# Moving the second attention's first tanh and a row turning into the last feed-forward chunk, and the way out of that chunk to another PSUM bank

## The chip, the cores and the metric

One NeuronCore of a Trainium2 chip runs the whole program. The metric is the device time of one execution in microseconds (us), as the median of several runs; smaller is better. The engines are named as the profile names them: PE (TensorE matmul), PEld (its weight loads), ACT (ScalarE), DVE (VectorE), POOL (GpSimd) and SP (SyncE, which issues the DMAs). Each engine works through its own instruction list strictly in the order in which the kernel wrote it, and engines meet only at semaphores.

## The reference

Input x is 2 x 1024 rows of 128. Four blocks follow one another, each of the form `x = x + layernorm(block(layernorm(x)))`:

1. block A, causal attention of one head with rotary embedding;
2. block B, a feed-forward of width 512: `h = silu(x w1) * (x w2)`, `h = gelu(h h1)`, `h = gelu(h h2)`, `out = h w3`, each product with a scale per output column;
3. block C, the second attention, of 8 heads, with two score maps L1 and L2 for each head:

```
G  = tanh(gain * (L1 - L2))
A1 = softmax(L1 + G)
A2 = softmax(L2 - G)
y  = rmsnorm((A1 - lambda * A2) @ v) * weight;  out = y @ Wo.T + bo
```

4. block D, a feed-forward with 8 routed experts.

## The kernel before, in words

Everything is written out by hand, engine by engine; no planner reorders anything. The 2048 rows are 16 tiles of 128, in 4 chunks of 512.

**Block B** runs over chunks c = 0 to 3. PE makes the first pair of products (L761), the product with h1 (L780), and the product with h2 (L790). The h2 product has four output tiles o = 0 to 3, each summed over k = 0 to 3 and each in PSUM bank o. ACT takes each tile o out with a Gelu (L1101, semaphore `g2_b`). Then `b_out_tile` (L747) multiplies with w3, one of four row tiles k4 at a time (T0 to T3 below), and DVE takes the four out together with `b_evac` (L1393, semaphore `yo_b`). For the last chunk the four tiles stand among the first products of block C, in bank 6. `c_prep_turn` turns the normed rows of chunk 2 for block C's projections and `c_evac` (ACT, L1047) takes them out of the turning bank, bank 7.

**Block C** is 128 steps, s = 0 to 127 (16 pairs of batch and head, n, by 8 key tiles, mt). A step consists of

- D(s), `c_diff`: two products of gain * q and k into banks 0 and 1, which give gain * (L1 - L2). It waits for tanh(s-1), which empties the banks;
- tanh(s), `tanh_step` on ACT, L1117, out of banks 0 and 1. It waits for D(s);
- F(s), `c_first`, into banks 2 and 3, and S(s), `c_second`, into banks 4 and 5: the two score maps. They wait for Zf(s-1) and Zs(s-1);
- Zf(s), `z_first` on DVE, L1486, adds tanh(s) to F(s), and Zs(s), `z_second`, L1491, takes tanh(s) from S(s), both into one of two halves of `zz`;
- exp(s) on ACT, L1146, 2048 columns of `zz`, waits for Zs(s);
- V(s), `c_values` on PE, L693: eight products of exp(s) with v, summed in bank 6. It waits for exp(s).

F, S and D all stand at L674 in the profile. The order within the loop of step s is, on PE, `D(s+3), turning, F(s+2), V(s), S(s+2)`; on ACT, `tanh(s+2), exp(s)`; on DVE, `Zf(s), Zs(s)` and then other work of that step. A preamble on PE fills the pipe. In the kernel before it reads, after the h2 product of the last chunk: `D(0), F(0), S(0), c_prep_turn(2), T0, D(1), T1, D(2), F(1), T2, S(1), T3`. ACT does, after the last Gelu, a small Exp (which brings the load of another function table, L1133), tanh(0), `c_evac(2)`, tanh(1), and then the loop.

`SPECIAL` is a table of further work in bank 7, by (n, mt). PE makes it before F(s+2) of that step, and DVE takes it out at the end of the following step (`turn_out`, L1505 for the kind "raw"). DVE's own list has `b_evac(3)` in step 1 and `b_stats(3)` (L1248 and L1251, four tiles each) in step 2. V(0) waits for `b_evac(3)`, since both use bank 6.

SP issues the loads of head 0 in the order q_g, k_s, q_s (semaphore `load[0]`), k_w, q_w (`cross[0]`), two DMAs each. D(0) waits for `load[0]`.

Of the kernel before, what the change touches and what calls it, by code (L numbers as in the profile page):

```python
# [27 lines left out]
BT = SEQ // P  # L28
# [41 lines left out]
SPECIAL = {(0, 2): ("raw", 0), (0, 5): ("raw", 1), (1, 1): ("v", 0), (1, 3): ("sums", 0), (2, 1): ("scale", 0),  # L70
# [72 lines left out]
def sandwich(nc, x_in, a_w, rope, b_w12, b_h1, b_h2, b_w3, b_s, b_s3, c_w, c_wo, c_bo, small,  # L143
             d_wg, d_wu, d_wd, d_wr, ident_in, ident_bf_in, mask_in, before_in, out):
    with ExitStack() as ctx:
# [342 lines left out]
        def _(pe):  # L488
# [128 lines left out]
            def c_turning(use):  # L617
# [3 lines left out]
                if kind == "o":  # L621
                    pe.wait_ge(S["accout"], i + 1)
                    last = turn_chunk(acc_sb.rearrange("p (a b) -> p a b", a=CT))
                elif kind == "late turn":
                    pe.wait_ge(S["xn_c"], CHUNKS)
                    last = turn_chunk(xn_c)
                elif kind == "raw":
                    if i == 0:
                        pe.wait_ge(S["xt_c"], CHUNKS - 1)
                    last = c_raw(i % 2, turn)  # L630
                elif kind == "v":
                    last = c_v()
                elif kind == "sums":
                    pe.wait_ge(S["sq_c"], CHUNKS - 1 + i)
                    last = c_sums(turn)
                elif kind == "scale":
                    pe.wait_ge(S["fac_c"], CHUNKS - 1 + i // 2)
                    last = c_scale(i % 2, turn)
                elif kind == "y":
                    pe.wait_ge(S["yc"], i + 1)  # L640
                    last = turn_chunk(y_c[i % 2])
                elif kind == "wo":
                    if i == 0:
                        pe.wait_ge(S["small_c"], 1)
# [106 lines left out]
            pe.wait_ge(ld["bw"], 48)  # L751
            for c in range(CHUNKS):
# [32 lines left out]
                for o in range(KT_):  # L785
                    pe.wait_ge(S["g1_b"], KT_ * c + o + 1)
                    for k in range(KT_):
                        if o == 0:
                            pe.wait_ge(S["g1_b"], KT_ * c + k + 1)
                        last = mm(ps[:, o, :], w_h2[:, k, o * P:(o + 1) * P], hid[:, 1, k, :],  # L790
                                  start=(k == 0), stop=(k == KT_ - 1))
                    last.then_inc(S["m2_b"], 1)
                    if 1 <= c < CHUNKS - 1:
# [62 lines left out]
            pe.wait_ge(load[0], 16 * OWN)  # L856
            late_c = CHUNKS - 1
            pe.wait_ge(S["g2_b"], KT_ * late_c + 2)
            c_diff(0, 0, 0)
            pe.wait_ge(cross[0], 16 * CROSSED)  # L860
            pe.wait_ge(S["g2_b"], KT_ * CHUNKS)
            c_first(0, 0, 0)
            pe.wait_ge(S["yo_b"], late_c)
            c_second(0, 0, 0)
            c_prep_turn(late_c - 1)
            pe.wait_ge(S["qh_c"], 2)
            b_out_tile(late_c, 0, ps[:, 6, :])
            c_diff(1, 0, 1)
            b_out_tile(late_c, 1, ps[:, 6, :])
            c_diff(2, 0, 2)  # L870
            c_first(1, 0, 1)
            b_out_tile(late_c, 2, ps[:, 6, :])
            c_second(1, 0, 1)
            b_out_tile(late_c, 3, ps[:, 6, :]).then_inc(S["y_b"], 1)
            for n in range(NH):
                for mt in range(BT):
                    s = n * BT + mt
                    later = s + 2 < NH * BT
# [19 lines left out]
                    if mt == 0:  # L898
                        pe.wait_ge(S["vh"], n + 1)
                        pe.wait_ge(S["accout"], n)  # L900
                        if n == 0:
                            pe.wait_ge(S["yo_b"], CHUNKS)
                    c_values(s, n % 2, mt)
                    if later:
                        c_second(s + 2, n2 % 2, mt2)

# [37 lines left out]
        def _(act):  # L944
# [129 lines left out]

            act.wait_ge(ld["bw"], 48)
            me.mark(A(tiny[:, 57:58], s_b[:, 0:1], ACT.Silu))
            for c in range(CHUNKS):
# [19 lines left out]
                for o in range(KT_):  # L1097
# [3 lines left out]
                    A(hid[:, 2, o, :], ps[:, o, :], ACT.Gelu, scale=s_b[:, 12 + o:13 + o]).then_inc(S["g2_b"], 1)  # L1101
                    if 1 <= c < CHUNKS - 1:
# [9 lines left out]

            def tanh_step(s, u, mt):
                act.wait_ge(S["dd"], s + 1)
                if s >= 3:
                    act.wait_ge(S["z2"], s - 2)
                A(gg[s % 3], banks[:, 0:2 * CHUNK], ACT.Tanh).then_inc(S["g"], 1)  # L1117
# [16 lines left out]
            tanh_step(0, 0, 0)  # L1134
            c_evac(CHUNKS - 2)
            tanh_step(1, 0, 1)
            for n in range(NH):
                for mt in range(BT):
                    s = n * BT + mt
                    if s + 2 < NH * BT:  # L1140
                        n2, mt2 = divmod(s + 2, BT)
                        tanh_step(s + 2, n2 % 2, mt2)
                    act.wait_ge(S["z2"], s + 1)
                    if s == NH * BT - 1:
                        act.wait_ge(S["av"], s - 1)
# [66 lines left out]
        def _(dve):  # L1212
# [435 lines left out]
            for n in range(NH):  # L1648
                u = n % 2
                for mt in range(BT):  # L1650
                    at = (n, mt)
                    z_first(n * BT + mt, mt)
                    if mt == 1 and n:
                        acc_out(n - 1)
                    z_second(n * BT + mt, mt)
                    if at == (0, 1):
                        b_evac(CHUNKS - 1, ps[:, 6, :])
# [5 lines left out]
                    if at == (0, 2):  # L1663
# [446 lines left out]
```

## Time and profile before

| what | value |
|---|---|
| median of 3 runs | 700.99 us (700.08 to 701.39) |
| the profiled execution, its time | 701.4 us |
| its span (first to last instruction) | 699.6 us |
| mean granted TensorE clock | 0.997 |
| PE busy | 633.5 us, 91% of the span |
| DVE busy | 529.0 us, 76% |
| ACT busy | 489.2 us, 70% |
| POOL busy | 188.2 us, 27% |

The profile shows one execution; times in it count from the first instruction. The execution took 701.4 us around a span of 699.6 us, so 1.8 us lie outside the span. The last chunk of block B ends on PE at about 234.1 us, and block C's steps run from there to about 599 us.

### The profile page before, as it was taken

The numbers are of one execution on the slowest core, as the hardware profiler recorded it, in microseconds if no ns is written. First come the engines' busy times: TensorE is split into PE (matmuls) and PEld (weight loads), VectorE is DVE, ScalarE is ACT, GpSimd is POOL, SyncE is SP. The second block draws the span as 40 slices with busy tenths as digits, with TensorE's granted clock in tenths as the row PEclk, the third lists the DMA queues.
The fourth block names the chain that finished last, engine by engine and source line by source line (L and its number), as shares of the span: only waits on it lengthen the run. The fifth ranks groups of instructions, "written<-read, shape, count | busy, mean of one in ns | idle before, by whom it ended". The sixth has DMA issues, their size and how long they took to land.

```text
span 699.6 us, 9403 instructions
## 1 busy us (share of the span) xinstructions
PE 633.5 (91%) x3324; PEld 272.5 (39%) x3324; DVE 529.0 (76%) x993; ACT 489.2 (70%) x504; POOL 188.2 (27%) x250
## 2 busy tenths in 40 slices
PE   8899999999999999889988888898898778899996
PEld 4677445464464423223321212122232111266555
DVE  5877603327054399999899999999999999676775
ACT  4657424234333699999999999999999989444432
POOL 3532340112102042491138101705500006022012
PEclk9999999999999999999999999999999999999999
DMA  6340200002205310244013420121101103300171
GB/s 172 102 171 1 92 1 0 2 0 72 64 1 147 101 33 26 57 115 135 9 49 111 138 58 21 37 57 57 38 20 58 56 3 121 120 1 1 47 226 30
DMA packets 33231, 44.60 MB, mean 64 GB/s; under 512 B 5409, under 2 KB 20001, under 8 KB 32801
## 3 DMA queue, kind: packets, MB, share of 16 engines
q1 hardware_dynamic: 33184, 44.01, 21.2%
q8 instruction: 26, 0.43, 0.3%
q14 instruction: 21, 0.16, 0.1%
HBM read 31.60 MB, written 10.55 MB: 60 GB/s over the span
## 4 chain that ended last, share of the span: by engine, by line
PE 39%; ACT 24%; DVE 23%; issue 11%; DMA 1%; POOL 1%; SPq 0%; DVEq 0%; ACTq 0%
ACT w_hh L1146 19%; PE ps L780 8%; PE ps L790 8%; DVE hid L1491 6%; DVE hid L1486 5%; PE ps L815 4%; PE ps L761 4%; PE ps L693 3%; PE ps L674 2%; ACT probs L1117 2%; PE ps L824 2%; DVE st L1248 2%; PE ps L747 2%; DMA x_res<-in_x 1%; PE ps L587 1%
## 5 line engine op out<-in xcount | busy, mean ns | idle before, releaser
L1146 ACT ACTIVATE w_hh<-hid 128x2048 f32<-128x2048 f32 x128 | 249.7, 1951 | 8.7 <-DVE hid L1491 8.2
L693 PE MATMUL ps<-w_hh,v_h 128*32 128x512 f32 x1024 | 137.3, 608 | 31.9 <-ACT w_hh L1146 30.3
L1486 DVE TENSOR_TENSOR hid<-ps,probs 128x1024 f32<-128x1024 f32 x86 | 104.5, 1215 | 19.7 <-ACT probs L1117 16.1
L674 PE MATMUL ps<-q_s,k_s 64*128 64x512 bf16 x256 | 99.0, 387 | 15.7 <-DVE hid L1486 15.1
L1491 DVE SCALAR_TENSOR_TENSOR hid<-ps,probs 128x1024 f32<-128x1024 f32 x86 | 104.7, 1217 | 4.7 <-PE ps L674 3.4
L674 PE MATMUL ps<-q_w,k_w 64*128 64x512 bf16 x256 | 99.0, 387 | 0.0
L1117 ACT ACTIVATE probs<-ps 128x1024 f32<-128x1024 f32 x86 | 91.1, 1059 | 1.9 <-PE ps L674 1.9
L674 PE MATMUL ps<-q_g,k_s 128*128 128x512 bf16 x256 | 77.9, 386 | 0.5 <-ACT probs L1117 0.5
L674 PEld LDWEIGHTS ps<-q_w,k_w 64*128 64x128 bf16 x256 | 23.7, 93 | 106.6 <-issue 53.6
L790 PE MATMUL ps<-hid,w_hh 128*128 128x512 f32 x128 | 56.3, 592 | 0.0
L780 PE MATMUL ps<-hid,w_hh 128*128 128x512 f32 x128 | 55.8, 594 | 0.0
L1491 DVE SCALAR_TENSOR_TENSOR hid<-ps,qkv_a 128x1024 f32<-128x1024 f32 x42 | 51.1, 1218 | 1.9 <-PE ps L674 1.5
L1486 DVE TENSOR_TENSOR hid<-ps,qkv_a 128x1024 f32<-128x1024 f32 x42 | 51.0, 1215 | 0.9 <-PE ps L674 0.2
L1181 ACT ACTIVATE q_g<-ps 128x512 f32<-128x512 f32 x32 | 19.0, 598 | 45.8 <-PE ps L815 45.6
L674 PEld LDWEIGHTS ps<-q_s,k_s 64*128 64x128 bf16 x256 | 23.7, 92 | 64.2 <-DVE hid L1486 36.1
L693 PEld LDWEIGHTS ps<-w_hh,v_h 128*32 128x32 f32 x1024 | 20.7, 108 | 67.9 <-ACT w_hh L1146 48.8
L1830 POOL TENSOR_SCALAR rs<-mv 128x4 f32<-128x4 f32 x18 | 5.5, 307 | 150.8 <-DVE mv L1251 150.8
L1117 ACT ACTIVATE qkv_a<-ps 128x1024 f32<-128x1024 f32 x42 | 44.5, 1060 | 1.2 <-PE ps L674 1.2
L1388 DVE SCALAR_TENSOR_TENSOR hid<-ps,s_b,rot 128x512 f32<-128x512 f32 x16 | 12.0, 751 | 39.6 <-ACT rot L1083 39.6
L1101 ACT ACTIVATE hid<-ps,s_b 128x512 f32<-128x512 f32 x16 | 11.0, 687 | 43.9 <-PE ps L790 43.9
L1899 POOL TENSOR_SCALAR v_h<-v_c 128x128 f32<-128x128 f32 x16 | 8.5, 534 | 113.6 <-PE ps L693 113.5
L780 PEld LDWEIGHTS ps<-hid,w_hh 128*128 128x128 f32 x128 | 24.0, 190 | 30.2 <-issue 29.4
(316 smaller groups left out, 1001.7 us busy)
## 6 DMA issues: line engine op xcount, KB each, us to landing
qk_rows<-part SPq DMA_DIRECT2D x48, 128.0 KB, 2.4
w_hh<-w_rows SPq DMA_DIRECT2D x4, 1024.0 KB, 8.9
qk_rows<-part_g SPq DMA_DIRECT2D x24, 128.0 KB, 2.4
q_g<-qk_rows SPq DMA_DIRECT2D x32, 96.0 KB, 2.2
k_s<-qk_rows SPq DMA_DIRECT2D x32, 96.0 KB, 2.3
q_s<-qk_rows SPq DMA_DIRECT2D x32, 96.0 KB, 2.4
k_w<-qk_rows SPq DMA_DIRECT2D x32, 96.0 KB, 2.5
q_w<-qk_rows SPq DMA_DIRECT2D x32, 96.0 KB, 2.4
```

Of the source, the lines that this page charges most:

```text
L674: last = mm(ps[:, base + half, :], k_op[rows, u, keys], q_op[rows, u, half * CHUNK:(half + 1) * CHUNK], start=True, stop=True)
L693: last = mm(ps[VW * g4:VW * g4 + VW, 6, :], v_h[:, u, mt, :], ee[:, mt % 2, g4 * CHUNK:(g4 + 1) * CHUNK], start=(mt == 0), stop=(mt == BT ...
L747: last = mm(bank[:, k4 * P:(k4 + 1) * P], hid[:, 2, k, k4 * P:(k4 + 1) * P], w_3[:, k, :], start=(k == 0), stop=(k == KT_ - 1))
L761: last = mm(ps[:, 2 * (m % 2) + w, :], w_12[:, w, m * P:(m + 1) * P], xt[:], start=True, stop=True)
L780: last = mm(ps[:, o, :], w_h1[:, k, o * P:(o + 1) * P], hid[:, 0, k, :], start=(k == 0), stop=(k == KT_ - 1))
L790: last = mm(ps[:, o, :], w_h2[:, k, o * P:(o + 1) * P], hid[:, 1, k, :], start=(k == 0), stop=(k == KT_ - 1))
L815: last = mm(ps[:, 2 * (n % 2) + w, :], wt[:, e, :], xt_d[c], start=True, stop=True)
L1117: A(gg[s % 3], banks[:, 0:2 * CHUNK], ACT.Tanh).then_inc(S["g"], 1)
L1146: A(ee[:, mt % 2, :], zz[:, mt % 2, :], ACT.Exp).then_inc(S["e"], 1)
L1181: A(sg_d[:, n % 2, :], ps[:, 2 * (n % 2), :], ACT.Silu).then_inc(S["sg_d"], 1)
L1486: v.tensor_tensor(zz[:, mt % 2, 0:SEQ], banks[:, 2 * CHUNK:4 * CHUNK], gg[s % 3], ALU.add).then_inc(S["z1"], 1)
L1491: v.scalar_tensor_tensor(zz[:, mt % 2, SEQ:2 * SEQ], banks[:, 4 * CHUNK:6 * CHUNK], -1.0, gg[s % 3], ALU.mult, ALU.subtract).then_inc(S["z ...
```

## The change

On PE, D(0) moves into the h2 product of the last chunk, behind (o, k) = (2, 2), with its wait for the loads and for the Gelu of tile 1. `c_prep_turn(2)` moves behind tile o = 2. On ACT, a small Exp and tanh(0) follow the Gelu of tile 1, and `c_evac(2)` follows the Gelu of tile 2. T0 to T3 go to the turning bank, bank 7, and `b_evac(3)` reads there. PE's preamble is a new order and now covers steps 0 and 1 of the loop as well, which the loop skips. After the h2 product it reads:

`S(0), D(1), F(0), T0, F(1), D(2), S(1), T1, F(2), V(0), S(2), D(3), F(3), T2, V(1), S(3), D(4)`, then the loop from s = 2, with T3 at the end of s = 2.

On ACT, exp(0) comes before tanh(2), and waits for both halves of Z(0). On DVE, Zs(0) comes before Zf(0), `b_evac(3)` moves from step 1 to step 3, `b_stats(3)` from step 2 to step 4. The "raw" turnings move from (0, 2) and (0, 5) to (0, 4) and (0, 6), and the first waits for `b_evac(3)`.

```diff
-SPECIAL = {(0, 2): ("raw", 0), (0, 5): ("raw", 1), (1, 1): ("v", 0), (1, 3): ("sums", 0), (2, 1): ("scale", 0),
+SPECIAL = {(0, 4): ("raw", 0), (0, 6): ("raw", 1), (1, 1): ("v", 0), (1, 3): ("sums", 0), (2, 1): ("scale", 0),
...
                     if i == 0:
                         pe.wait_ge(S["xt_c"], CHUNKS - 1)
+                        pe.wait_ge(S["yo_b"], CHUNKS)
...
                         last = mm(ps[:, o, :], w_h2[:, k, o * P:(o + 1) * P], hid[:, 1, k, :],
                                   start=(k == 0), stop=(k == KT_ - 1))
+                        if (c, o, k) == (late_c, 2, 2):
+                            pe.wait_ge(S["g2_b"], KT_ * late_c + 2)
+                            pe.wait_ge(load[0], 16 * OWN)
+                            c_diff(0, 0, 0)
                     last.then_inc(S["m2_b"], 1)
+                    if (c, o) == (late_c, 2):
+                        c_prep_turn(late_c - 1)
...
-            pe.wait_ge(load[0], 16 * OWN)
-            late_c = CHUNKS - 1
-            pe.wait_ge(S["g2_b"], KT_ * late_c + 2)
-            c_diff(0, 0, 0)
             pe.wait_ge(cross[0], 16 * CROSSED)
+            pe.wait_ge(S["yo_b"], late_c)
+            pe.wait_ge(S["qh_c"], 2)
+            c_second(0, 0, 0)
+            c_diff(1, 0, 1)
             pe.wait_ge(S["g2_b"], KT_ * CHUNKS)
             c_first(0, 0, 0)
-            pe.wait_ge(S["yo_b"], late_c)
-            c_second(0, 0, 0)
-            c_prep_turn(late_c - 1)
-            pe.wait_ge(S["qh_c"], 2)
-            b_out_tile(late_c, 0, ps[:, 6, :])
-            c_diff(1, 0, 1)
-            b_out_tile(late_c, 1, ps[:, 6, :])
+            pe.wait_ge(S["xt_c"], late_c)
+            b_out_tile(late_c, 0, turn)
+            c_first(1, 0, 1)
             c_diff(2, 0, 2)
-            c_first(1, 0, 1)
-            b_out_tile(late_c, 2, ps[:, 6, :])
             c_second(1, 0, 1)
-            b_out_tile(late_c, 3, ps[:, 6, :]).then_inc(S["y_b"], 1)
+            b_out_tile(late_c, 1, turn)
+            c_first(2, 0, 2)
+            pe.wait_ge(S["vh"], 1)
+            c_values(0, 0, 0)
+            c_second(2, 0, 2)
+            c_diff(3, 0, 3)
+            c_first(3, 0, 3)
+            b_out_tile(late_c, 2, turn)
+            c_values(1, 0, 1)
+            c_second(3, 0, 3)
+            c_diff(4, 0, 4)
             for n in range(NH):
                 for mt in range(BT):
                     s = n * BT + mt
+                    if s < 2:
+                        continue
...
-                        if n == 0:
-                            pe.wait_ge(S["yo_b"], CHUNKS)
                     c_values(s, n % 2, mt)
                     if later:
                         c_second(s + 2, n2 % 2, mt2)
+                    if s == 2:
+                        b_out_tile(late_c, 3, turn).then_inc(S["y_b"], 1)
...
                     A(hid[:, 2, o, :], ps[:, o, :], ACT.Gelu, scale=s_b[:, 12 + o:13 + o]).then_inc(S["g2_b"], 1)
+                    if (c, o) == (CHUNKS - 1, 1):
+                        me.mark(A(tiny[:, 58:59], tiny[:, 0:1], ACT.Exp))
+                        tanh_step(0, 0, 0)
+                    if (c, o) == (CHUNKS - 1, 2):
+                        c_evac(CHUNKS - 2)
...
             me.mark(A(tiny[:, 56:57], tiny[:, 0:1], ACT.Exp))
-            tanh_step(0, 0, 0)
-            c_evac(CHUNKS - 2)
             tanh_step(1, 0, 1)
             for n in range(NH):
                 for mt in range(BT):
                     s = n * BT + mt
-                    if s + 2 < NH * BT:
+                    if 0 < s < NH * BT - 2:
                         n2, mt2 = divmod(s + 2, BT)
                         tanh_step(s + 2, n2 % 2, mt2)
                     act.wait_ge(S["z2"], s + 1)
+                    if s == 0:
+                        act.wait_ge(S["z1"], 1)
                     if s == NH * BT - 1:
                         act.wait_ge(S["av"], s - 1)
                     A(ee[:, mt % 2, :], zz[:, mt % 2, :], ACT.Exp).then_inc(S["e"], 1)
+                    if s == 0:
+                        tanh_step(2, 0, 2)
...
                     at = (n, mt)
+                    if at == (0, 0):
+                        dve.wait_ge(S["g"], 1)
+                        z_second(0, 0)
                     z_first(n * BT + mt, mt)
                     if mt == 1 and n:
                         acc_out(n - 1)
-                    z_second(n * BT + mt, mt)
-                    if at == (0, 1):
-                        b_evac(CHUNKS - 1, ps[:, 6, :])
+                    if at != (0, 0):
+                        z_second(n * BT + mt, mt)
+                    if at == (0, 3):
+                        b_evac(CHUNKS - 1, turn)
...
-                    if at == (0, 2):
+                    if at == (0, 4):
                         b_stats(CHUNKS - 1)
```

## Rows read from the trace of the kernel before

**Rows 1.** The page, costliest groups: count | busy, mean ns | idle before, releaser

```profile
L1146 ACT ACTIVATE w_hh<-hid 128x2048 f32<-128x2048 f32 x128 | 249.7, 1951 | 8.7 <-DVE hid L1491 8.2
```

**Rows 2.** The chain that ended last, 234 to 262 us: start, us, what

```profile
237.90 1.03 ACT probs L1117
...
241.36 1.22 DVE hid L1491
...
246.01 0.87 DVE st L1248 x4
```

**Rows 3.** Timeline at the last h2 product: start, us, instruction

```profile
220.15 13.90 PE L790 MATMUL ps<-hid,w_hh 128*128 128x512 f32 x32
...
227.22 0.69 ACT L1101 ACTIVATE hid<-ps,s_b 128x512 f32<-128x512 f32 x1 [2.75 <-PE ps L790]
...
234.09 0.69 ACT L1101 ACTIVATE hid<-ps,s_b 128x512 f32<-128x512 f32 x1 [2.75 <-PE ps L790]
234.79 1.28 ACT L1133 ACT_TABLE_LOAD   x1
...
237.10 0.59 ACT L1047 ACTIVATE xt_c<-ps 128x512 f32<-128x512 f32 x1
```

**Rows 4.** Issues of q_s for head 0 on SP's queue, and their landing

```profile
227.22 0.90 SPq L426 DMA_DIRECT2D q_s<-qk_rows  x2
...
DMA to landing us min/median/max: 2.3/2.4/2.4
```

**Rows 5.** Timeline of block C's first steps, 239 to 264 us

```profile
239.51 0.39 PE L674 MATMUL ps<-q_s,k_s 64*128 64x512 bf16 x1
...
240.02 1.23 DVE L1486 TENSOR_TENSOR hid<-ps,probs 128x1024 f32<-128x1024 f32 x1 [0.43 <-PE ps L674]
240.54 1.90 ACT L1146 ACTIVATE w_hh<-hid 128x2048 f32<-128x2048 f32 x1
...
240.93 0.39 PE L674 MATMUL ps<-q_w,k_w 64*128 64x512 bf16 x1
...
241.25 1.16 PE L747 MATMUL ps<-w,hid 128*128 128x128 f32 x8
...
242.24 0.59 PE L674 MATMUL ps<-q_g,k_s 128*128 128x512 bf16 x2
242.50 0.68 DVE L1393 TENSOR_TENSOR y<-ps,s 128x512 f32<-128x512 f32 x1
...
242.87 1.03 ACT L1117 ACTIVATE probs<-ps 128x1024 f32<-128x1024 f32 x1 [0.43 <-PE ps L674]
...
243.44 1.07 PE L693 MATMUL ps<-w_hh,v_h 128*32 128x512 f32 x8 [0.28 <-DVE y L1393]
243.79 1.90 ACT L1146 ACTIVATE w_hh<-hid 128x2048 f32<-128x2048 f32 x1
...
244.44 0.39 PE L674 MATMUL ps<-q_w,k_w 64*128 64x512 bf16 x1
...
247.21 1.19 DVE L1486 TENSOR_TENSOR hid<-ps,probs 128x1024 f32<-128x1024 f32 x1
...
249.44 0.67 DVE L1505 COPY raw<-ps 128x512 f32<-128x512 f32 x1
...
252.41 1.91 ACT L1146 ACTIVATE w_hh<-hid 128x2048 f32<-128x2048 f32 x1
...
254.23 1.01 ACT L1117 ACTIVATE probs<-ps 128x1024 f32<-128x1024 f32 x1
...
263.25 1.92 ACT L1146 ACTIVATE w_hh<-hid 128x2048 f32<-128x2048 f32 x1
```

**Rows 6.** Stretches late in block C: us, busy of each engine, then granted clock

```profile
555.00:558.00 3.00, 0.88 (x7) 0.16 (x4) 2.90 (x5) 2.53 (x2) 0.00 (x0) 1.00 0.00 0
558.00:561.00 3.00, 2.97 (x13) 0.54 (x14) 2.37 (x3) 1.86 (x1) 0.00 (x0) 0.56 0.00 0
...
570.00:573.00 3.00, 1.79 (x13) 0.46 (x14) 3.00 (x4) 1.90 (x3) 0.00 (x0) 1.00 0.00 0
```

More of the change, by code:

```diff
@@ L751, in _ @@
             pe.wait_ge(ld["bw"], 48)
+            late_c = CHUNKS - 1
             for c in range(CHUNKS):
@@ L1073, in c_gained_middle, with tanh_step @@
                 A(part_g[:, 1, :], g_q[:], ACT.Copy).then_inc(S["gmid_c"], 1)
+            def tanh_step(s, u, mt):
+                act.wait_ge(S["dd"], s + 1)
+                if s >= 3:
+                    act.wait_ge(S["z2"], s - 2)
+                A(gg[s % 3], banks[:, 0:2 * CHUNK], ACT.Tanh).then_inc(S["g"], 1)
             act.wait_ge(ld["bw"], 48)
@@ L1110, in _ @@
                     A(tiny[:, 8:17], tiny[:, 8:17], ACT.Tanh).then_inc(S["fact_c"], 1)
[L1113 to L1117, printed above, removed]
             def d_gate(b):
```

## The prediction

> **What bounds the kernel now.** I read the page first, for what fills the stretch behind the change. The 128 exps of block C take 249.7 us of ACT, which hardly ever waits for them [rows 1]. So what counts is when each exp starts, and above all when the even rhythm begins. I number exps by step. Then I read the chain that ended last from 234 us, to see who is late at the start. It passes from ACT's tanh chain (tanh(1) at 237.90) to DVE (Zs(1) at 241.36) and stays with DVE through `b_stats` at 246.01 [rows 2]. Last came the timeline of the two stretches. At the end of block B PE runs without a gap: 32 instructions in 13.7 us of distance, so 3.43 us for each tile o and 0.86 us for each k. The last Gelu starts at 234.09 and the table load for Exp and Tanh at 234.79 [rows 3]. In block C exp(0) starts at 240.54, exp(1) at 243.79, exp(4) at 252.41 and exp(8) at 263.25 [rows 5]. From exp(4) on that is (263.25 - 252.41) / 4 = 2.71 us a step, 1.82 us from an exp to the next tanh and 0.90 us from there to the next exp [rows 5]: ACT alone, with nobody waited for. A delay at exp(4) to exp(8) therefore moves everything behind it, since every later transfer and turning is started by a step, and not by the clock.
>
> **Prices.** All from rows 5 unless named. F or S costs PE 0.3 us (S(1) 240.93 to the tile product 241.25). A tile product T costs 1.0 (241.25 to 242.24), V 1.0 (243.44 to 244.44). From D's start to its tanh 0.63 (242.24 to 242.87); from F's or S's start to its Z 0.45 to 0.5 (239.51 to 240.02, and S(1) at 240.93 to 241.36 [rows 2]). A Z takes 1.22 and hands over to the next after 1.14. `b_evac` is 0.68, `b_stats` 1.2 (246.01 [rows 2] to 247.21), a raw copy 0.67.
>
> **The part inside block B.** Product (2, 2) of the last chunk would end at 220.32 + 11 x 0.86 = 229.8. The second q_s load is issued at about 227.7 and lands 2.4 later, at 230.1 [rows 4]. So PE, with tile 2's last product, tile 3 and everything else queued behind it, stands for about 0.35 us. D(0) adds 0.45 (half to 0.6 us bound it) and the turning 0.45, both between products that ran gap free. The h2 product ends at 234.06 + 1.25 = 235.3 instead of 234.1. ACT has time for its part: Gelu of tile 1 ends at 227.9, table load to 229.2, tanh(0) 230.8 to 231.9, load back to 233.2, Gelu of tile 2 to 233.9, `c_evac` to 234.4 (0.59 [rows 3]). The last Gelu waits for PE alone, 235.4 to 236.1, load to 237.4, small Exp 0.1, tanh(1) at 237.5. The two added loads cost nothing as long as ACT is free by 235.4, which leaves 1.0 us.
>
> The row for the load is 1.28 us, starting 0.01 us after the Gelu's end [rows 3]. The Trainium skill (ScalarE: Activation LUTs, "What ACT_TABLE_LOAD costs") prices a switch of table sets at about 2.66 us, with a drain behind the load. By that price the Gelu of tile 2 would start 1.4 us later, at 234.6, and `c_evac` would end at 235.8, so the last Gelu would lose about 0.4 us.
>
> **exp(0) comes earlier.** S(0) at 235.4, D(1) at 235.7, F(0) after the last Gelu at 236.1. Zs(0) 235.9, Zf(0) 237.0 to 238.2. tanh(1) 237.5, exp(0) at 238.4 (0.9 after it), against 240.54: 2.1 us gained. This is tanh(0) out of the chain, and tanh(2) behind exp(0).
>
> **Then PE's order gives it back.** In the loop of before, D(s+3) stands ahead of V(s). In the new preamble D(3) stands behind V(0), and D(4) behind V(1). V(s) waits for exp(s), and ACT's next instruction is a tanh that waits for that D.
>
> - exp(0) ends at 240.3. PE by then has F(1) 238.25 (waits for Zf(0)), D(2) 238.6, S(1) 239.0, T1 239.3, F(2) 240.3. V(0) 240.6, S(2) 241.6, D(3) 241.9. tanh(2) ends at 241.3, so ACT waits from there to tanh(3) at 242.55. exp(1) 243.45. Against 243.79: of the 2.1 us 0.35 is left.
> - exp(1) ends 245.35, V(1) 245.4, S(3) 246.4, D(4) 246.7, tanh(4) 247.35, exp(2) 248.25. Without the wait tanh(4) would come 1.82 after exp(1), at 245.27; this is the new stall, 2.1 us, of which ACT stands idle for 2.0. Behind D(4) on PE stands D(5), which needs tanh(4) finished (248.4), then F(4) and V(2). Before, exp(2) came at 243.79 + 2.71 = 246.50. Now 1.75 late.
>
> **And T3 holds DVE.** T3 stands behind V(2) and S(4). exp(2) ends 250.15, V(2) 250.2, S(4) 251.2, T3 251.5 to 252.6. DVE has finished Zs(3) at about 248.1 and stands in `b_evac(3)`, in order, so Zf(4) and Zs(4) queue behind it. `b_evac` 252.65, Zf(4) 253.35, Zs(4) 254.5 to 255.7, exp(4) 255.7. ACT alone would have had exp(3) at 251.0 and exp(4) at 254.1 (tanh(6) waits 0.4 for D(6), behind T3). So DVE adds 1.6. Against 252.41: 3.3 late.
>
> DVE is now the bound and its other work comes next: `b_stats` 255.6, Zf(5) 256.8, Zs(5) to 259.15, exp(5) 259.2, against 252.41 + 2.71 = 255.12: 4.05 late. Raw copy 259.1, Z(6) 259.7 to 262.0, exp(6) 262.05 (ACT alone 261.9): 4.2 late. Z(7) ends 264.3, before ACT wants it at 264.75. Raw copy again, Z(8) ends 267.15, exp(8) 267.45 against 263.25: **4.2 late**. After that DVE gains 2.71 - 2.28 = 0.43 us a step. PE is not in the way: F and S of these steps are each there 0.2 us or more before their Z. POOL's norm of the last chunk starts 10 us later than before and must have ended for DVE's step 18 only, some 30 us on.
>
> Sum: -2.1 (exp(0)) + 1.75 (wait before tanh(3) and the work before left out) + 2.1 (wait before tanh(4)) = 1.75; + 1.6 (T3 and `b_evac`) = 3.3; + 0.9 (`b_stats` and raw copy now exposed) = 4.2. The profiled execution would go from 701.4 to 705.6 (span 699.6 to 703.8). It lies 0.4 above the median of the runs, so the median comes to 700.99 + 4.2 = **705.2 us**. Rounding over this many steps, PE's handling of the wait in block B (0.35, bounded by nothing and 1 us), and one more delay at the head change (0 to 0.5) give 704.2 to 706.4 for this case.
>
> **The rivals.**
>
> *A. Only the two D waits cost.* If T3 were done when DVE comes to `b_evac`, or if DVE's lead over ACT took it up, exp(4) would be at 254.1, and `b_stats` and the raw copies would be mostly hidden: 1.7 to 2.3 late, 702.7 to 703.3. Against it: T3 cannot start before exp(2) has ended and Zs(3) does not depend on exp(2). 0.10.
>
> *B. Faster: the early exp(0) is kept.* It decides by whether a D is ready when ACT comes to tanh(3) and tanh(4). If PE got through V(0), S(2) and D(3) within the 0.9 us that tanh(2) takes, and V(1), S(3) and D(4) before exp(1)'s successor, nothing would be late: 2.1 us of gain less a `b_evac` wait of at most 1, so 699 to 700. Row by row V alone takes 1.0, more than tanh's 0.9 to 1.03, and it cannot overlap its own exp. 0.05.
>
> *C. Nothing to measure.* The stretch is about 30 us; if the four delays came out half as large they would be about 1.2 us net. 0.05.
>
> *D. The clock falls.* Late in block C a stretch of 3 us with PE busy for 0.88 us was followed by one granted 0.56, near the lower of the two levels (1.2 and 2.4 GHz); another with 1.79 of 3 kept 1.00 [rows 6]. My PE has waits of up to 1.6 us here (behind T2, behind D(4), behind D(6)), so about 1.5 busy in 3, between those two rows. At the lower clock a V costs 2 instead of 1 us, on the chain: 1 to 2 us more, 706.2 to 707.2. The Trainium skill (TensorE: Matmul & The Clock Gate, "The HAM clock gate") says that the chip halves this clock after an idle stretch and gives it back on activity; the granted clock above agrees. 0.12.
>
> **How the numbers follow.** Main case 0.68; A 0.10, B 0.05, C 0.05, D 0.12. Within 0.2% (1.4 us, about what a measurement of this kernel can tell from no change) lie C and nearly half of B. Slower: 0.90, same 0.07, faster 0.03. The range for 8 in 10 reaches from A's edge to D's: 702.8 to 706.9.
>
> **What would show it.** In the profile after: D(0) among L790 near 230 us with a wait for a DMA ahead of it; three table loads between 227 and 238; exp(0) near 238.4 and exp(1) near 243.5; ACT idle about 1.2 us before tanh(3) and 2.1 before tanh(4), released by PE L674; DVE idle some 4.5 us before L1393, released by PE L747; exp(8) near 267.5 and then 2.71 a step. I am wrong if tanh(4) follows exp(1) without a wait, if L1393 starts before 251, or if the offset of later exps (the tail of the span too) is not that of exp(8).

## The result and the profile after

The changed kernel takes **706.12 us** (median of 4 runs, 705.37 to 707.42) against 700.91 us for the kernel before (4 runs, 700.08 to 701.39). The ratio is 1.0077 with a 95% interval of 1.0061 to 1.0093: slower by 5.2 us. Forecast were 705.2 us and a range of 702.8 to 706.9.

The page of the changed kernel: first the busy times, then two of the costliest groups with the idle time before them.

```profile
span 703.6 us, 9373 instructions
...
PE 628.2 (89%) x3289; PEld 272.2 (39%) x3324; DVE 529.1 (75%) x993; ACT 492.2 (70%) x507; POOL 188.7 (27%) x250
...
L1165 ACT ACTIVATE w_hh<-hid 128x2048 f32<-128x2048 f32 x128 | 249.8, 1952 | 10.9 <-DVE hid L1512 10.5
...
L1093 ACT ACTIVATE probs<-ps 128x1024 f32<-128x1024 f32 x86 | 91.3, 1061 | 6.3 <-PE ps L675 6.3
```

ACT's busy time grew by 3.0 us, mostly two table loads, but no other engine has more work, and the exps take what they took [rows 1]. What grew is ACT's waiting: 10.9 us before exps, against 8.7 in the kernel before, and 6.3 us before these tanhs, against 1.9. So the time went into waits, and the timeline says where. First the part inside block B (L792 is the h2 product, L675 is D, F or S, L1121 the Gelu, L1093 a tanh):

```profile
225.69 3.17 PE L792 MATMUL ps<-hid,w_hh 128*128 128x512 f32 x7
226.32 0.69 ACT L1121 ACTIVATE hid<-ps,s_b 128x512 f32<-128x512 f32 x1 [2.75 <-PE ps L792]
227.03 1.28 ACT L1123 ACT_TABLE_LOAD   x1
...
229.51 0.13 PEld L675 LDWEIGHTS ps<-q_g,k_s 128*128 128x128 bf16 x2 [1.48 <-issue]
229.76 0.38 PE L675 MATMUL ps<-q_g,k_s 128*128 128x512 bf16 x1 [0.90 <-issue]
...
229.97 1.02 PE L792 MATMUL ps<-hid,w_hh 128*128 128x512 f32 x2
...
230.17 1.03 ACT L1093 ACTIVATE probs<-ps 128x1024 f32<-128x1024 f32 x1 [1.64 <-PE ps L675]
...
231.21 1.28 ACT L1121 ACT_TABLE_LOAD   x1
...
232.51 0.69 ACT L1121 ACTIVATE hid<-ps,s_b 128x512 f32<-128x512 f32 x1
...
234.90 0.69 ACT L1121 ACTIVATE hid<-ps,s_b 128x512 f32<-128x512 f32 x1 [1.22 <-PE ps L792]
```

This execution reached the end of block B's last chunk with a head start of 0.90 us over that of before: the Gelu of tile 1 starts at 226.32 and not at 227.22 [rows 3]. To compare two traces I therefore count from that Gelu, "Gelu 1". The last Gelu comes 8.58 us after Gelu 1, against 6.87 [rows 3]: 1.71 late.

The bracket of 0.90 us in front of D(0) is too long. D(0) is two products, and the trace has the record of one of them only (x1). The weights of both were loaded at 229.51, and product (2, 3) follows at 229.97. In experiment 10 both records are there, D(0) starts at 229.50, and product (2, 3) follows 0.43 us later, at 229.93. So D(0) started at about 229.54 here, and PE stood for some 0.68 us, an estimate from these rows. Counted in the distance from one product to the next, the h2 product lost 1.71 us: 0.43 for D(0) (229.54 to 229.97), 0.43 for the turning, and 0.85 for the stall.

ACT has 1.22 us to spare before the last Gelu, so the added loads cost nothing. Then block C (L1165 is exp, L1507 and L1512 are Zf and Zs, L694 is V, L748 a tile product, L1414 `b_evac`):

```profile
237.91 1.90 ACT L1165 ACTIVATE w_hh<-hid 128x2048 f32<-128x2048 f32 x1
...
240.34 1.07 PE L694 MATMUL ps<-w_hh,v_h 128*32 128x512 f32 x8
...
242.30 1.02 ACT L1093 ACTIVATE probs<-ps 128x1024 f32<-128x1024 f32 x1 [1.57 <-PE ps L675]
...
243.22 1.90 ACT L1165 ACTIVATE w_hh<-hid 128x2048 f32<-128x2048 f32 x1
245.18 1.06 PE L694 MATMUL ps<-w_hh,v_h 128*32 128x512 f32 x8 [1.50 <-ACT w_hh L1165]
...
246.50 0.61 PE L675 MATMUL ps<-q_g,k_s 128*128 128x512 bf16 x2
...
247.14 1.02 ACT L1093 ACTIVATE probs<-ps 128x1024 f32<-128x1024 f32 x1 [2.01 <-PE ps L675]
248.06 1.90 ACT L1165 ACTIVATE w_hh<-hid 128x2048 f32<-128x2048 f32 x1
...
251.33 1.16 PE L748 MATMUL ps<-w,hid 128*128 128x128 f32 x8
...
252.53 0.69 DVE L1414 TENSOR_TENSOR y<-ps,s 128x512 f32<-128x512 f32 x1 [4.70 <-PE ps L748]
...
255.51 1.91 ACT L1165 ACTIVATE w_hh<-hid 128x2048 f32<-128x2048 f32 x1 [1.53 <-DVE hid L1512]
...
258.94 1.91 ACT L1165 ACTIVATE w_hh<-hid 128x2048 f32<-128x2048 f32 x1 [0.61 <-DVE hid L1512]
```

Read the brackets downward. ACT waits 1.57 us for D(3), which stands behind V(0), then 2.01 us for D(4), which stands behind V(1). DVE stands 4.70 us in front of `b_evac`, released by T3, and Zf(4) and Zs(4) queue behind it; ACT pays 1.53 us of that at exp(4), and 0.61 at exp(5), in front of which DVE also does `b_stats`. The next step takes 2.86 us, and after that they are 2.71 us apart. exp(8) is at 267.23.

| start | predicted | less the 0.90 of this execution | measured |
|---|---|---|---|
| last Gelu | 235.4 | 234.5 | 234.90 |
| exp(0) | 238.4 | 237.5 | 237.91 |
| exp(1) | 243.45 | 242.55 | 243.22 |
| exp(2) | 248.25 | 247.35 | 248.06 |
| exp(4) | 255.7 | 254.8 | 255.51 |
| exp(8) | 267.45 | 266.55 | 267.23 |

exp(8) comes 40.91 us after Gelu 1, against 36.03 before (263.25 - 227.22 [rows 3, 5]): 4.88 us late. The spans differ by 4.0, which is 4.88 less the 0.90 of the head start.

### The profile page after: what moved, and what is told of

Same layout as the page of the kernel before. It is cut to its first block, busy times and chain, and to the rows that moved or that the text cites. A ratio compares the mean times of both kernels' runs of the same rounds, so it can differ in the third digit from the quotient of the medians.

```text
span 703.6 us, 9373 instructions
## 1 busy us (share of the span) xinstructions
PE 628.2 (89%) x3289; PEld 272.2 (39%) x3324; DVE 529.1 (75%) x993; ACT 492.2 (70%) x507; POOL 188.7 (27%) x250
## 4 chain that ended last, share of the span: by engine, by line
PE 39%; DVE 24%; ACT 23%; issue 11%; DMA 1%; POOL 1%; SPq 0%; DVEq 0%; ACTq 0%
ACT w_hh L1165 18%; PE ps L782 8%; PE ps L792 8%; DVE hid L1512 6%; DVE hid L1507 6%; PE ps L823 4%; PE ps L763 4%; PE ps L694 3%; PE ps L675 3%; PE ps L832 2%; PE ps L748 2%; DVE st L1269 2%; ACT probs L1093 2%; PE ps L587 1%; DMA x_res<-in_x 1%
## 5 line engine op out<-in xcount | busy, mean ns | idle before, releaser
L1165 ACT ACTIVATE w_hh<-hid 128x2048 f32<-128x2048 f32 x128 | 249.8, 1952 | 10.9 <-DVE hid L1512 10.5
L694 PE MATMUL ps<-w_hh,v_h 128*32 128x512 f32 x1024 | 137.0, 607 | 33.2 <-ACT w_hh L1165 32.2
L1512 DVE SCALAR_TENSOR_TENSOR hid<-ps,probs 128x1024 f32<-128x1024 f32 x86 | 104.8, 1218 | 19.4 <-PE ps L675 18.3
L675 PE MATMUL ps<-q_s,k_s 64*128 64x512 bf16 x256 | 99.3, 388 | 17.6 <-DVE hid L1507 17.4
L1507 DVE TENSOR_TENSOR hid<-ps,probs 128x1024 f32<-128x1024 f32 x86 | 104.7, 1217 | 5.4 <-ACT w_hh L1165 2.1
L675 PE MATMUL ps<-q_w,k_w 64*128 64x512 bf16 x256 | 99.3, 388 | 0.0
L1093 ACT ACTIVATE probs<-ps 128x1024 f32<-128x1024 f32 x86 | 91.3, 1061 | 6.3 <-PE ps L675 6.3
L675 PE MATMUL ps<-q_g,k_s 128*128 128x512 bf16 x221 | 69.8, 385 | 7.6 <-issue 6.3
L675 PEld LDWEIGHTS ps<-q_w,k_w 64*128 64x128 bf16 x256 | 23.6, 92 | 107.5 <-DVE hid L1512 54.2
L792 PE MATMUL ps<-hid,w_hh 128*128 128x512 f32 x128 | 56.6, 592 | 0.0
L1512 DVE SCALAR_TENSOR_TENSOR hid<-ps,qkv_a 128x1024 f32<-128x1024 f32 x42 | 51.2, 1219 | 1.5 <-PE ps L675 1.2
L1507 DVE TENSOR_TENSOR hid<-ps,qkv_a 128x1024 f32<-128x1024 f32 x42 | 51.1, 1217 | 1.4 <-DVE rs L1653 0.3
L675 PEld LDWEIGHTS ps<-q_s,k_s 64*128 64x128 bf16 x256 | 23.6, 92 | 65.7 <-DVE hid L1507 39.1
L694 PEld LDWEIGHTS ps<-w_hh,v_h 128*32 128x32 f32 x1024 | 20.6, 108 | 69.1 <-ACT w_hh L1165 49.7
L1093 ACT ACTIVATE qkv_a<-ps 128x1024 f32<-128x1024 f32 x42 | 44.6, 1061 | 0.5 <-PE ps L675 0.5
L1121 ACT ACTIVATE hid<-ps,s_b 128x512 f32<-128x512 f32 x16 | 11.0, 687 | 39.6 <-PE ps L792 39.6
```

The lines of the kernel that those rows point to most:

```text
L675: last = mm(ps[:, base + half, :], k_op[rows, u, keys], q_op[rows, u, half * CHUNK:(half + 1) * CHUNK], start=True, stop=True)
L694: last = mm(ps[VW * g4:VW * g4 + VW, 6, :], v_h[:, u, mt, :], ee[:, mt % 2, g4 * CHUNK:(g4 + 1) * CHUNK], start=(mt == 0), stop=(mt == BT ...
L1507: v.tensor_tensor(zz[:, mt % 2, 0:SEQ], banks[:, 2 * CHUNK:4 * CHUNK], gg[s % 3], ALU.add).then_inc(S["z1"], 1)
L1512: v.scalar_tensor_tensor(zz[:, mt % 2, SEQ:2 * SEQ], banks[:, 4 * CHUNK:6 * CHUNK], -1.0, gg[s % 3], ALU.mult, ALU.subtract).then_inc(S["z ...
```

## Experiments

All but the first two rows are timed in five rounds beside the kernel before on the same chip; the ratio is not exactly that of the two medians. "exp(8) - Gelu 1" and "exp(8) - exp(0)" are in us, from the one profile of each kernel, so they are free of what happens earlier in the execution. The second is free of the stall in front of D(0) too. That stall is not the same in each execution: exp(0) comes 11.32 to 11.59 us after Gelu 1 in the seven profiles of kernels that are the same up to there and have D(0) behind (2, 2).

| kernel | median us | before us | ratio (95%) | exp(8) - Gelu 1 | exp(8) - exp(0) |
|---|---|---|---|---|---|
| before | | | | 36.03 | 22.71 |
| changed | 706.12 | 700.91 | 1.0077 (1.0061 to 1.0093) | 40.91 | 29.32 |
| D(3), D(4) first | 703.07 | 700.51 | 1.003 (1.0018 to 1.0043) | 37.98 | 26.66 |
| T3 early | 702.70 | 700.51 | 1.0027 (1.0017 to 1.0037) | 37.96 | 26.50 |
| both | 700.33 | 700.51 | 0.9994 (0.9983 to 1.0005) | 35.38 | 24.02 |
| block B part alone | 701.32 | 700.51 | 1.0012 (1.0003 to 1.0021) | 37.02 | 22.71 |
| both, D(0) one product later | 699.35 | 700.26 | 0.9984 (0.9976 to 0.9993) | 34.78 | 24.03 |
| both, nothing in block B | 702.28 | 700.26 | 1.0024 (1.0015 to 1.0033) | 36.50 | 24.04 |
| changed, `b_evac` in step 4 | 704.30 | 700.26 | 1.0058 (1.0045 to 1.0072) | 40.07 | 28.64 |
| changed, D(0) one product later | 704.75 | 700.26 | 1.0064 (1.0051 to 1.0077) | 41.63 | 30.88 |
| changed, T2 repeated | 705.06 | 701.35 | 1.006 (1.0044 to 1.0076) | 40.68 | 29.31 |
| changed, again | 707.24 | 701.35 | 1.0086 (1.0071 to 1.0101) | 42.34 | 30.89 |

### 1. D(3) and D(4) ahead of V(0) and V(1)

```diff
             c_first(2, 0, 2)
+            c_diff(3, 0, 3)
             pe.wait_ge(S["vh"], 1)
             c_values(0, 0, 0)
             c_second(2, 0, 2)
-            c_diff(3, 0, 3)
             c_first(3, 0, 3)
             b_out_tile(late_c, 2, turn)
+            c_diff(4, 0, 4)
             c_values(1, 0, 1)
             c_second(3, 0, 3)
-            c_diff(4, 0, 4)
```

> The changed kernel with D(3) put ahead of V(0) and D(4) ahead of V(1), as the loop has it. Theory (PE's order starves ACT's tanh): the wait before tanh(4) of 2.0 us falls to about 0.3 and the one before tanh(3) from 1.6 to about 0.7; T3 still stands behind V(2), so DVE still idles some 3 us in front of b_evac; exp(4) comes 2.7 us earlier relative to the last Gelu, time about 703.4. Rival (the loss is made inside block B, by PE's stall and the two added table loads, and the order only shifts idle time about): no change, about 706.

Measured 703.07 us. The timeline, tanh(3), tanh(4), `b_evac` and exp(4):

```profile
241.74 1.02 ACT L1093 ACTIVATE probs<-ps 128x1024 f32<-128x1024 f32 x1 [0.70 <-PE ps L675]
...
244.79 1.02 ACT L1093 ACTIVATE probs<-ps 128x1024 f32<-128x1024 f32 x1 [0.23 <-PE ps L675]
...
250.18 0.69 DVE L1414 TENSOR_TENSOR y<-ps,s 128x512 f32<-128x512 f32 x1 [2.84 <-PE ps L748]
...
253.17 1.91 ACT L1165 ACTIVATE w_hh<-hid 128x2048 f32<-128x2048 f32 x1 [1.53 <-DVE hid L1512]
```

The two waits went from 1.57 to 0.70 and from 2.01 to 0.23, 2.65 us together. exp(8) came 2.93 us earlier after Gelu 1, of which 0.27 was there at exp(0) already (a shorter stall in front of D(0)), so the order is worth 2.66. DVE's wait on T3 stayed, at 2.84 us, and so did the 1.53 us that ACT pays for it. The rival, that the order only shifts idle time, is out.

### 2. T3 alone, into PE's idle time

```diff
             b_out_tile(late_c, 2, turn)
+            b_out_tile(late_c, 3, turn).then_inc(S["y_b"], 1)
             c_values(1, 0, 1)
...
-                    if s == 2:
-                        b_out_tile(late_c, 3, turn).then_inc(S["y_b"], 1)
```

> The changed kernel with only T3 moved, right behind T2, into the 1.5 us for which PE idles before V(1). Theory: the waits before tanh(3) and tanh(4) stay (1.6 and 2.0 us), DVE's idle time of 4.7 us before b_evac is gone, Zf(4) starts when exp(2) ends, b_stats and raw copies are mostly hidden; exp(4) 2.0 us and exp(8) 2.7 us earlier, about 703.4. Rival (the D waits are the whole loss and DVE's wait is in their shadow): exp(4) at most 0.4 earlier, 705.7 or more.

Measured 702.70 us. tanh(4) and `b_evac` in its timeline:

```profile
247.35 1.02 ACT L1092 ACTIVATE probs<-ps 128x1024 f32<-128x1024 f32 x1 [2.02 <-PE ps L675]
247.96 0.68 DVE L1413 TENSOR_TENSOR y<-ps,s 128x512 f32<-128x512 f32 x1
```

`b_evac` follows Zs(3) with no wait, tanh(4) waits as in the changed kernel, and exp(8) is 2.95 us earlier, 2.82 counted from exp(0). So T3 behind V(2) costs 2.8 us in the changed kernel. From exp(2) to exp(4) the two profiles differ by 2.04 us, from exp(4) to exp(5) by 0.73, where DVE has no lead to hide `b_stats`, and from there to exp(8) by 0.04. The raw copies cost next to nothing more than they do here. The rival, that the waits for D are the whole loss, is out.

### 3. Both

The edit of experiment 1, and T3 here:

```diff
             c_values(1, 0, 1)
             c_second(3, 0, 3)
+            b_out_tile(late_c, 3, turn).then_inc(S["y_b"], 1)
...
-                    if s == 2:
-                        b_out_tile(late_c, 3, turn).then_inc(S["y_b"], 1)
```

> Both: D(3) and D(4) ahead of V(0) and V(1), T3 behind S(3). Theory: no wait over 0.7 us on ACT after exp(1), exp(8) 5.4 us earlier than in the changed kernel relative to the last Gelu, about 700.7, that is within half a us of the kernel before. If the two are one and the same loss, no better than the better of the two alone, 703.4.

Measured 700.33 us; counted from exp(0), exp(8) is 5.30 us earlier than in the changed kernel, against 2.66 + 2.82 = 5.48 for the two alone. The two losses are separate and add up to within 0.2 us. With both gone the median equals that of the kernel before within its interval, though in the profile exp(8) comes 0.65 us earlier after Gelu 1 than before (35.38 against 36.03).

### 4. Only the part inside block B

The kernel before, with D(0), tanh(0), the turning and its way out put among the h2 products as in the change, and nothing else.

Against the kernel before:

```diff
+                        if (c, o, k) == (late_c, 2, 2):
+                            pe.wait_ge(S["g2_b"], KT_ * late_c + 2)
+                            pe.wait_ge(load[0], 16 * OWN)
+                            c_diff(0, 0, 0)
                     last.then_inc(S["m2_b"], 1)
+                    if (c, o) == (late_c, 2):
+                        c_prep_turn(late_c - 1)
...
-            pe.wait_ge(load[0], 16 * OWN)
-            late_c = CHUNKS - 1
-            pe.wait_ge(S["g2_b"], KT_ * late_c + 2)
-            c_diff(0, 0, 0)
...
-            c_prep_turn(late_c - 1)
...
+                    if (c, o) == (CHUNKS - 1, 1):
+                        me.mark(A(tiny[:, 58:59], tiny[:, 0:1], ACT.Exp))
+                        tanh_step(0, 0, 0)
+                    if (c, o) == (CHUNKS - 1, 2):
+                        c_evac(CHUNKS - 2)
...
-            tanh_step(0, 0, 0)
-            c_evac(CHUNKS - 2)
             tanh_step(1, 0, 1)
```

> The kernel before with only the part inside block B: D(0), tanh(0), the turning and its way out among the h2 products; preamble, bank 6, DVE's and the table's order as before. Theory: the last Gelu comes 1.7 us later (stall 0.9, D 0.4, turning 0.4), tanh(1) waits for D(1) behind T0, exp(0) ends up some 0.9 later than before, 701.5 to 701.9. Rival (block B is where the loss is made): 704 or more.

Measured 701.32 us. PE in front of D(0), then ACT's last Gelu, tanh(1) and exp(0):

```profile
229.96 0.38 PE L674 MATMUL ps<-q_g,k_s 128*128 128x512 bf16 x1 [1.04 <-issue]
...
235.10 0.69 ACT L1109 ACTIVATE hid<-ps,s_b 128x512 f32<-128x512 f32 x1 [1.22 <-PE ps L791]
...
238.05 1.02 ACT L1081 ACTIVATE probs<-ps 128x1024 f32<-128x1024 f32 x1 [0.75 <-PE ps L674]
...
240.69 1.91 ACT L1151 ACTIVATE w_hh<-hid 128x2048 f32<-128x2048 f32 x1
```

(The 1.04 us is again in front of D(0)'s second product.) exp(0) is 14.31 us after Gelu 1 against 13.32 before (240.54 - 227.22 [rows 3, 5]), and from there to exp(8) it takes the 22.71 us of before. What tanh(0) saves behind the last Gelu is spent in block B and on waiting for D(1), which in this order stands behind T0. This part, by itself, is a loss of 1 us, not of 5; the median of 701.32 is a little under the 701.5 to 701.9 expected.

### 5. Both, and D(0) one product later

```diff
-                        if (c, o, k) == (late_c, 2, 2):
+                        if (c, o, k) == (late_c, 2, 3):
```

> The kernel with D(3), D(4) ahead of V(0), V(1) and T3 behind S(3), and D(0) one product later, behind (2, 3) of the h2 product, by when the loads of head 0 have landed. Theory: PE's stall of 0.7 us in block B is gone, the last Gelu and everything behind it come 0.6 us earlier, about 699.7 against 700.3 for the same kernel with D(0) behind (2, 2). Rival (the stall is hidden by ACT's table loads): no difference.

Measured 699.35 us, 0.16% under the kernel before with an interval that leaves out 1. The row of D(0), then the last Gelu:

```profile
230.05 0.38 PE L675 MATMUL ps<-q_g,k_s 128*128 128x512 bf16 x1
...
234.34 0.69 ACT L1120 ACTIVATE hid<-ps,s_b 128x512 f32<-128x512 f32 x1 [0.36 <-PE ps L792]
```

There is no wait in front of D(0), and the last Gelu comes 7.74 us after Gelu 1, against 8.35 with D(0) behind (2, 2) in the kernel with both. This is the version that beats both kernels. The gain is small, 0.9 us.

### 6. Both, with nothing in block B

D(0), tanh(0), the turning and `c_evac(2)` back behind the h2 product, and D(1), which needs tanh(0), one place later; otherwise as experiment 3.

The hunks of experiment 4 taken out again, and on PE behind the h2 product:

```diff
+            pe.wait_ge(load[0], 16 * OWN)
+            pe.wait_ge(S["g2_b"], KT_ * late_c + 2)
+            c_diff(0, 0, 0)
+            c_prep_turn(late_c - 1)
             pe.wait_ge(cross[0], 16 * CROSSED)
...
             c_second(0, 0, 0)
-            c_diff(1, 0, 1)
             pe.wait_ge(S["g2_b"], KT_ * CHUNKS)
             c_first(0, 0, 0)
+            c_diff(1, 0, 1)
             pe.wait_ge(S["xt_c"], late_c)
```

> The kernel with D(3), D(4) ahead of V(0), V(1) and T3 behind S(3), but D(0), tanh(0), the turning and c_evac(2) put back behind the h2 product. Theory: what block B's part costs PE (1.7 us) is about what it saves ACT behind the last Gelu; without it Z(0) waits for tanh(0) and exp(0) comes 0.8 us later, about 701.1 against 700.3. Rival (the part inside block B is a net loss, by two added table loads and the stall): 699.5 or less.

Measured 702.28 us, 1.2 more than expected, but in two groups: four of 12 executions took 700.6 to 701.05 us, all at a mean granted clock of 0.998, and eight took 701.9 to 703.3 us, at 0.993 to 0.996. The profiled one is of the first group, at 701.05, as expected. So in the new order the part inside block B is worth having: exp(8) comes 1.1 us later without it (36.50 against 35.38), all of it before exp(0). Where the executions of the second group lose more was not profiled.

### 7. `b_evac` one step later on DVE alone

```diff
-                    if at == (0, 3):
+                    if at == (0, 4):
                         b_evac(CHUNKS - 1, turn)
```

> The changed kernel with b_evac(3) moved on DVE alone, from behind Zs(3) to behind Zs(4); PE's and ACT's orders as changed, T3 still behind V(2). Theory (Zf(4) and Zs(4) are held only because they queue behind b_evac): DVE's wait moves from 4.7 us on T3 to a short one on exp(2), exp(4) 1.4 us and exp(8) 2.0 us earlier, about 704.1. Rival (T3's time on PE is the cost, not the queue on DVE): no change, 706.

Measured 704.30 us. Zf(4), `b_evac`, exp(4), and the stretches of 3 us from 249 to 255 (the granted clock stands behind POOL's busy time):

```profile
251.34 1.23 DVE L1507 TENSOR_TENSOR hid<-ps,probs 128x1024 f32<-128x1024 f32 x1 [2.22 <-ACT w_hh L1165]
...
255.28 0.69 DVE L1414 TENSOR_TENSOR y<-ps,s 128x512 f32<-128x512 f32 x1 [0.24 <-PE ps L748]
...
256.64 1.90 ACT L1165 ACTIVATE w_hh<-hid 128x2048 f32<-128x2048 f32 x1
```

```profile
249.00:252.00 3.00, 1.62 (x8) 0.41 (x12) 0.78 (x2) 3.00 (x3) 0.00 (x0) 0.85 0.00 0
252.00:255.00 3.00, 3.00 (x18) 1.39 (x11) 1.75 (x2) 1.97 (x2) 0.00 (x0) 0.58 0.00 0
```

T3 stands where it stood in PE's list, only DVE's queue differs, and the wait of 4.70 us in front of `b_evac` became 0.24. exp(4), which waited 1.53 us for DVE, now follows its tanh at once. This profiled execution, the second longest of its kernel at 705.66 us, shows something else: PE was granted 0.85 and 0.58 of its clock while V(2), S(4) and T3 ran. That is rival D, and it is why exp(8) is only 0.84 us earlier than in the first profile of the changed kernel, and not 2.0.

The fair partner is experiment 10, the changed kernel in an execution with a like fall of the clock (0.70 and 0.73). In both, exp(3) comes 12.85 us after exp(0). Then tanh(6) waits 1.75 us here and 1.86 there, and exp(4) comes 17.43 us after exp(0) here and 19.18 there, exp(8) 28.64 and 30.89: 2.25 us earlier, with DVE's order alone changed. So most of the 2.8 us that T3 costs is the queue behind `b_evac`. The rest, some 0.6 us by these numbers, is left for its time on PE. The rival (only PE's time counts) is out.

### 8. The changed kernel with D(0) one product later

The edit of experiment 5, in the changed kernel as it is.

> The changed kernel with only D(0) one product later, behind (2, 3) of the h2 product. Theory: the stall of 0.9 us in front of D(0) is gone and nothing else changes; the last Gelu 0.7 us earlier, about 705.4 against 706.1.

Measured 704.75 us against the 706.12 of the changed kernel on another chip; the ratios, 1.0064 and 1.0077, differ by less than their intervals. In the profile exp(0) is 10.75 us after Gelu 1, against 11.59: 0.84 earlier, the stall. But its exp(8) is 41.63 after Gelu 1, later than the changed kernel's 40.91, for the clock fell here too (0.64 and 0.79 in the stretches from 249 to 255). From exp(0) to exp(8) it takes 30.88 us, against 30.89 in experiment 10, which has the fall, and 29.32 in the first profile, which has not.

### 9. and 10. The clock

The changed kernel once more, and beside it, on the same chip, the changed kernel with the tile product T2 made two more times, in two of PE's waits. The values are the same, so nothing of the result changes.

```diff
             b_out_tile(late_c, 2, turn)
+            b_out_tile(late_c, 2, turn)
             c_values(1, 0, 1)
             c_second(3, 0, 3)
             c_diff(4, 0, 4)
+            b_out_tile(late_c, 2, turn)
```

> The changed kernel with the tile product T2 repeated twice (same values into the same columns), once before V(1) and once behind D(4), both where PE waits over 1 us. It adds 2.0 us of work to PE, inside its waits. Theory (in some executions the clock falls to its lower level in the stretch 246 to 255 us, as PE stands too much, and V(2), S(4), T3 and D(6) on the chain take nearly twice their time): no execution grants less than 1.00 between 243 and 258, the median is 0.5 to 1 us below that of the changed kernel on the same chip, near 705.2, and the longest execution under 706.3. Rival (PE's idle time has nothing to do with it): same median and spread, or later by what the two products delay D(5).

> The changed kernel itself, on the same chip as the one with the repeated tile products. Theory: median near 706, executions from 705.0 to 707.5, the longer ones with the lower mean clock (0.994 against 0.997).

Measured 705.06 with T2 repeated and 707.24 without, on one chip. The stretches of the changed kernel in this second measurement, with D(0), V(2) and T3 in its timeline below:

```profile
243.00:246.00 3.00, 1.50 (x14) 0.60 (x12) 0.90 (x2) 2.08 (x2) 0.00 (x0) 1.00 0.00 0
246.00:249.00 3.00, 1.88 (x12) 0.42 (x8) 1.62 (x2) 1.91 (x2) 0.00 (x0) 1.00 0.02 5
249.00:252.00 3.00, 2.13 (x12) 0.26 (x10) 0.00 (x0) 3.00 (x3) 0.00 (x0) 0.70 0.00 0
252.00:255.00 3.00, 2.45 (x12) 1.75 (x10) 0.94 (x2) 1.14 (x2) 0.00 (x0) 0.73 0.00 0
```

```profile
229.50 0.59 PE L675 MATMUL ps<-q_g,k_s 128*128 128x512 bf16 x2 [0.54 <-issue]
...
249.97 1.76 PE L694 MATMUL ps<-w_hh,v_h 128*32 128x512 f32 x8 [0.87 <-ACT w_hh L1165]
...
252.20 1.82 PE L748 MATMUL ps<-w,hid 128*128 128x128 f32 x8
```

And with T2 repeated:

```profile
246.00:249.00 3.00, 2.77 (x22) 1.37 (x14) 2.08 (x2) 1.44 (x2) 0.00 (x0) 1.00 0.03 5
249.00:252.00 3.00, 2.13 (x16) 0.60 (x15) 0.00 (x0) 3.00 (x3) 0.00 (x0) 1.00 0.00 0
```

V(2) takes 1.76 us at the lower of the two levels (1.2 and 2.4 GHz) for most of it, against 1.07 at full clock, T3 1.82 against 1.16. exp(8) comes 42.34 us after Gelu 1 against 40.91 in the first profile of the same kernel, where the same stretches were granted 1.00. Counted from exp(0), which is free of the stall before D(0), it is 30.89 against 29.32: the fall costs 1.57 us. With T2 repeated the count is 29.31 us, that of the changed kernel without the fall, so the added products themselves cost nothing.

With 2 us of products more, the kernel was 2.2 us faster by the medians. The two profiled executions differ by 1.4 us (705.64 and 707.01). So the fall in this stretch can account for some 1.6 of the 2.2; where the rest comes from was not found. That the filling keeps the clock up is made likely by the times (four of five executions with it at 705.64 or less, none without it under 706.83) and by one profile, but the first profile of the changed kernel kept 1.00 with no filling.

Three parts of the expectations failed. The longest execution with T2 repeated took 707.01 and not under 706.3, and what it lost was not profiled. That no execution has the fall is known for the profiled one alone. And the changed kernel gave no short executions here: its median is 707.24 and not near 706, its longest 708.01.

All five executions of the changed kernel here showed 0.993 to 0.995 as the mean clock. But the mean does not tell where the clock fell. The profile of experiment 5 has 0.995 with 1.00 in all this stretch and a fall near 558 us (0.54), and the kernel before falls there too [rows 6]. So a mean of 0.994 in an execution that was not profiled does not show a fall at V(2).

## Why the prediction was right

**The direction and its two causes** were right and are shown, each by an experiment that took one away: PE's order starving tanh(3) and tanh(4) (2.66 us, experiment 1) and T3 with DVE's queue behind it (2.82 us, experiment 2). Set against the kernel before, the terms of the sum came out like this:

| stretch | in the sum | measured |
|---|---|---|
| up to exp(0), from Gelu 1 | -2.1 | -1.73 |
| exp(0) to exp(1) | +1.75 | +2.06 |
| exp(1) to exp(2) | +2.1 | +2.13 |
| exp(2) to exp(4) | +1.6 | +1.54 |
| exp(4) to exp(8) | +0.9 | +0.88 |
| together | 4.2 | 4.88 |

So the last three terms, among them the waits for D(4) and for T3, were right within 0.1 us, and the miss of 0.7 lies in the first two.

**The gain at exp(0)** was 0.4 us too large, because the stall in front of D(0) was sized at 0.35 us and cost 0.85 of distance. Three things make up the 0.5 us. The working counted the stall from the end of product (2, 2), 229.8, but the next product could have started about 0.2 earlier: the products start 0.43 us apart from 220.15 on [rows 3], which puts the one behind (2, 2) at 229.6. The last of the loads took 2.6 us to land and not 2.4, so it landed at 229.4 and not at 229.2 (230.1 less the 0.90 of this execution). And about 0.1 passed from there to the first product of D(0), at 229.54, for which there was no term. Experiments 5 and 8 gave the stall back (0.61 and 0.84 us). D(0) and the turning took 0.43 each, as priced.

**The other 0.3 us** arose between exp(0) and V(0), which is 2.43 us (237.91 to 240.34) where the working had 2.2. D(2) takes 0.54 us of PE up to S(1) (238.07 to 238.61) where 0.4 was counted, and T1 1.09 up to F(2) (238.93 to 240.02) and not 1.0.

**The table loads** were hidden, with 1.22 us to spare. The Gelu of tile 2 started 1.30 us after the start of the load before it (231.21 to 232.51), so 1.28 was the whole price. With D(0) one product later 0.36 us were still to spare (experiment 5). The Trainium skill (ScalarE: Activation LUTs, "What ACT_TABLE_LOAD costs") has 2.66; this trace does not bear it out, and the 0.4 us that followed from it did not appear.

**Rival A** (only the D waits cost) is out by experiment 2, **B** and **C** by the time. **Rival D, the clock,** I had priced at 1 to 2 us with a chance of 0.12. It was not a rival but an addition: in the first profiled execution it did not occur, in another of the same kernel it did, at a cost of 1.57 us, within the price given. Median 706.12 with executions up to 707.42 fits a mixture: 4.88 us from the waits, and part of the executions with the fall on top. How the four first executions divide was not profiled.

**Luck** had a part in how close the numbers came. The profiled execution took 705.37 us where 705.6 was forecast, but only because it started with 0.90 us of a head start that nobody forecast and then lost 0.68 more than the sum. The median, 706.12, is inside the bounds of the main case, 704.2 to 706.4, by 0.3 us. On the chip of experiment 10 the same kernel took 707.24 us, 5.9 above the kernel before there, which is more than the main case allowed.

Open: why one chip or execution has the fall and another not. The two profiles of the changed kernel show the same busy times of PE in the 6 us before it, 1.50 and 1.88 of 3 us each, and one fell and the other did not. In the profile of experiment 6 PE was busy for 1.20 us in the stretch from 234 to 237, and the clock stayed at 1.00.

## What to carry to other kernels

An instruction that waits for the current step, like V(s), should not stand on a queue ahead of one that feeds the next step of the bound engine, like D(s+3): the loop had this right, and the hand-written preamble that replaced two of its rounds lost it, for 2.7 us. When the order of one engine is rewritten, follow each of its products to the queue that consumes it; T3 cost little of its 2.8 us on PE, and most of it because `b_evac` stood ahead of Zf(4) on DVE. Moving work in under a busy engine pays only what that engine doesn't lose: with PE's order as in the kernel before it was a loss of 1.0 us at exp(8), with the better order it was worth 1.1 us, and 1.7 once no load was waited for. With the order of the changed kernel it was not tried apart.

When two profiles are compared, count from the last point before which both do the same, and compare only executions with the same granted clock in that stretch. Counted so, two kernels that differ in nothing that ACT waits for gave the same number within 0.02 us: 29.32 and 29.31 at full clock, 30.88 and 30.89 with the fall.

## What the runs showed that was not expected

The granted clock fell after waits of at most 1.5 us each. In the two stretches of 3 us before the fall PE was busy for 1.50 and 1.88 us; the fall came as V(2) started, and the next two stretches were granted 0.70 and 0.73. Filling two of the waits with work that nobody needs went with a kernel faster by 2.2 us on that chip, and with a clock of 1.00 in the profiled execution. The Trainium skill (TensorE: Matmul & The Clock Gate, "The HAM clock gate") says that idling lowers this clock and activity restores it; the direction agrees with these rows, though PE had waited for 1.5 us at most.
